# Two-network graph kernel on one core: the first LayerNorm with nodes on partitions, every reciprocal on columns of 25, the last LayerNorm's scale applied where be1 is added

## The chip, the core and the metric

One core of a Trainium2 chip. Five engines work side by side and meet by semaphores: TensorE (PE, matmul; its weight loads are listed as PEld), VectorE (DVE), ScalarE (ACT), GpSimd (POOL) and SyncE (SP, which here issues DMAs). SBUF and PSUM have 128 partitions. The metric is the device time of one execution in microseconds, the median of the runs.

## The reference

3125 nodes, 53125 edges sorted by destination, 128 features, all in float32. Cut to what is computed:

```
h = relu(layernorm(x))                                   # (x - mean) / sqrt(var + 1e-5), per node
for l in 1, 2, 3:                                        # three SAGE layers
    agg = segment_sum(h[src], dst) / max(count, 1)
    h = agg @ Wl.T + bl + h @ Wr.T                       # relu after layers 1 and 2
x = x + h
h = relu(layernorm(x))
messages = gelu((h[src] + edge_attr) @ We1 + be1) @ We2 + be2
u = (1 + eps) * h + segment_sum(messages, dst)
x = x + (gelu(u @ Wu1 + bu1) @ Wu2 + bu2)
```

## The kernel before

Node data lie transposed, features on the 128 partitions and the 3125 nodes along columns, in 7 chunks: six of 500 nodes and one of 125. A chunk has four blocks of 125 nodes (the last chunk has one), 25 blocks in all. Where rows of nodes are needed, 125 partitions hold one block.

The program has three stages.

**Build.** The dense matrix of edge counts `adj` (source node on partitions in blocks, destination along columns, 8 bits) is made from one-hots. 213 slots (`GB`) of two tiles of 125 edges each: DVE writes four one-hots (`key_onehots`, L444 to L459), PE multiplies them (`sum_group`, L720), ACT copies the result to `adj` (`keep_block`, L653). Before the first slot DVE works out the keys of all 425 tiles in ten operations (L429 to L442) that need `src_idx`, `dst_idx` and `firsts`. One-hots have 5 buffers, so DVE can be four slots ahead of PE; what DVE does in slot s of the plan is set against PE's slot s - 5 (`LEAD`).

**Dense layers.** A SAGE layer's sum over neighbours is `parts` (h as three bfloat16 parts, rows of nodes) times `adj`: 75 matmuls for each layer and chunk (`dense_unit`, L801). An order written out in `Plan` says in which slot each step of each chunk is issued on its engine. The first layer's matmuls are set among the slots of the build, 2.3 to a slot (`RATE`), from slot 38 on; after the build a slot is just nine of them. The result is multiplied by the reciprocal of the node's edge count (`mean_rows`, L492), mixed with weights on PE (`mix_layer`, L774), passed through ReLU on ACT (`activate`), turned by PE (`turn`, L753), and split: the high part by ACT (`split_high`, L673), the remainder by DVE (`split_rest`, L478), the middle and lowest parts by POOL (L402 to L405).

The counts: for each chunk SP stores the last partition's row of `adj` to DRAM and loads it as 25 rows (L354 to L360, with a wait between), PE sums it into all 128 partitions (`count`, L766), and DVE clips it and takes the reciprocal of [128 x 500] (`reciprocal_counts`, L485).

Both norms run on the transposed data: PE subtracts the mean by a matmul (`centre`, L737), ACT squares, PE averages the squares into all partitions (`variance`, L748), ACT takes the root, DVE the reciprocal of [128 x 500] and then max(., 0) times it (`normalise`, L470). The first norm is in slots 2 to 34 of the build. The last norm follows the third layer chunk by chunk: PE's `mix_rows` (h @ We1, rows of nodes, L788) waits for it, DVE adds `be1` (`keep_rows`, L509), and SP stores the rows to the `table` in DRAM (L365 to L370).

**Edges.** 85 groups of 625 edges. Once the table is stored, POOL gathers its rows with five indirect DMAs per group (L409 to L416), with 4 buffers: from group 4 on it waits for DVE's `pre` of four groups back. PE multiplies the edge features by We1, DVE adds the gathered rows (`pre`, L639), ACT takes GELU, DVE makes the window's one-hots, PE sums into the nodes (L895). Ahead of group 0 DVE runs checks of the input (`check_input`), which wait for the two loads of `order` (L371, L372) that SP issues right behind the table stores. PE waits for these checks at group 0 too. When a chunk's edges are done, `node_mix`, `node_sum`, `node_up`, `node_down` and `node_add` make its output.

## Time and profile before

| | |
|---|---|
| median of 3 runs | 1102.52 us (1101.01 to 1102.76) |
| the profiled execution | 1104.38 us, its span 1102.3 us |
| PE busy | 861.3 us, 78% of the span |
| DVE busy | 466.2 us, 42% |
| POOL busy | 443.8 us, 40% |
| ACT busy | 233.8 us, 21% |
| moved by DMA | 63.01 MB |

The span runs from the first to the last instruction; what lies around it is 2.1 us. Shares over the whole span mix the three stages, so they are to be read by stretches: the page cuts the span into 40 slices of 27.6 us and gives each engine's busy share in tenths. Operations of one engine overlap a little: the duration of one is longer than the distance from its start to the next one's start.

A row of a timeline gives the start, the duration (both us), the engine, the line of the kernel, the operation with output <- input, and in brackets the engine's idle time before it and what ended that. A row of a group gives line, engine, operation, shapes and count, then the busy time of all (us) and the mean of one (ns), then the idle time of the engine just before them. A row of a DMA queue gives packets, MB and the time they took as a share of 16 engines over the stretch.

### The profile page before, as it was taken

The numbers are of one execution on the slowest core, as the hardware profiler recorded it, in microseconds if no ns is written. First come the engines' busy times: TensorE is split into PE (matmuls) and PEld (weight loads), VectorE is DVE, ScalarE is ACT, GpSimd is POOL, SyncE is SP. The second block draws the span as 40 slices with busy tenths as digits, with TensorE's granted clock in tenths as the row PEclk, the third lists the DMA queues.
The fourth block names the chain that finished last, engine by engine and source line by source line (L and its number), as shares of the span: only waits on it lengthen the run. The fifth ranks groups of instructions, "written<-read, shape, count | busy, mean of one in ns | idle before, by whom it ended". The sixth has DMA issues, their size and how long they took to land.

```text
span 1102.3 us, 13178 instructions
## 1 busy us (share of the span) xinstructions
PE 861.3 (78%) x4419; PEld 601.1 (55%) x4419; DVE 466.2 (42%) x1522; ACT 233.8 (21%) x378; POOL 443.8 (40%) x483
## 2 busy tenths in 40 slices
PE   2658898999999998878756687586687687677576
PEld 1334454445544454434456686575676676666475
DVE  5999999994100012232363223223323323323221
ACT  1535666663100000000101111111111111111111
POOL 1110000000010100000077777777777777777773
PEclk9867999999999999998856557758657658567756
DMA  4000000001000000000033333333334333334321
GB/s 118 0 1 2 2 3 2 2 2 48 1 1 1 1 1 10 10 9 11 16 102 107 111 96 113 111 100 120 99 100 120 100 100 120 104 107 119 101 76 38
DMA packets 34768, 63.01 MB, mean 57 GB/s; under 512 B 10189, under 2 KB 16891, under 8 KB 34696
## 3 DMA queue, kind: packets, MB, share of 16 engines
q1 hardware_dynamic: 19224, 32.24, 9.8%
q0 software_dynamic: 13600, 27.88, 8.8%
q10 hardware_dynamic: 1872, 1.99, 0.6%
q8 instruction: 37, 0.61, 0.2%
q14 instruction: 35, 0.29, 0.1%
HBM read 58.80 MB, written 3.28 MB: 56 GB/s over the span
## 4 chain that ended last, share of the span: by engine, by line
POOL 36%; PE 34%; DVE 14%; issue 12%; DMA 2%; ACT 1%; POOLq 0%; SPq 0%; ACTq 0%; DVEq 0%
POOL f_adj L413 36%; PE f_ps L813 24%; DVE f_region L454 2%; PE f_ps L733 2%; DVE f_region L473 2%; DVE f_work L473 2%; DVE f_region L458 2%; PE f_ps L726 2%; DVE f_region L452 2%; DVE f_rcntT L490 1%; PE f_ps L785 1%; PE f_ps L786 1%; DVE f_region L456 1%; DMA f_adj<-in_firsts 1%; PE f_ps L797 1%
## 5 line engine op out<-in xcount | busy, mean ns | idle before, releaser
L413 POOL DMA_INDIRECT f_adj<-table,f_src_idx x425 | 403.7, 950 | 283.3 <-DMA table<-f_region 154.1
L813 PE MATMUL f_ps<-f_adj,f_parts 125*128 125x500 fp8e4 (+1 forms) x1575 | 341.2, 358 | 0.0
L895 PE MATMUL f_ps<-f_adj 125*128 125x101 f32 (+19 forms) x1020 | 207.0, 375 | 144.0 <-ACT f_adj L713 144.0
L895 PEld LDWEIGHTS f_ps<-f_adj 125*128 125x128 f32 x1020 | 192.8, 288 | 169.4 <-issue 168.9
L813 PEld LDWEIGHTS f_ps<-f_adj,f_parts 125*128 125x128 bf16 x1575 | 145.6, 99 | 136.6 <-issue 22.3
L554 DVE TENSOR_SCALAR f_adj<-f_iota,f_dst_abs 125x101 f32<-125x101 f16 (+3 forms) x425 | 87.0, 291 | 264.8 <-PE f_ps L895 264.7
L844 PE MATMUL f_ps<-f_We,f_region 128*125 128x128 f32 x850 | 178.4, 384 | 0.5 <-DVE f_region L514 0.5
L844 PEld LDWEIGHTS f_ps<-f_We,f_region 128*125 128x125 f32 x850 | 167.0, 294 | 0.7 <-issue 0.7
L403 POOL CAST f_parts<-f_rest 125x512 bf16<-125x512 f32 (+1 forms) x21 | 12.4, 590 | 356.6 <-DVE f_rest L483 356.6
L713 ACT ACTIVATE f_adj<-f_adj 125x640 f32<-125x640 f32 x85 | 62.6, 736 | 422.1 <-DVE f_adj L639 422.1
L659 ACT CAST f_adj<-f_ps 128x500 f32 x213 | 125.9, 591 | 86.1 <-PE f_ps L733 75.1
L639 DVE TENSOR_TENSOR f_adj<-f_ps,f_adj 125x640 f32<-125x640 f32 x85 | 69.8, 821 | 90.9 <-issue 69.6
L726 PE MATMUL f_ps<-f_region 125*128 125x300 f16 (+1 forms) x213 | 67.1, 315 | 39.7 <-DVE f_region L458 38.9
L733 PE MATMUL f_ps<-f_region 125*128 125x375 f16 x212 | 72.8, 343 | 0.0
L454 DVE TENSOR_SCALAR f_region<-f_iota,f_key 125x375 f16<-125x375 f16 x212 | 71.8, 338 | 0.0
L452 DVE TENSOR_SCALAR f_region<-f_iota,f_key 125x300 f16<-125x300 f16 x212 | 65.1, 307 | 5.9 <-PE f_ps L733 5.2
L726 PEld LDWEIGHTS f_ps<-f_region 125*128 125x128 f16 x213 | 21.8, 102 | 75.4 <-issue 47.4
L458 DVE TENSOR_SCALAR f_region<-f_iota,f_low 125x126 f16<-125x126 f16 x213 | 60.9, 286 | 0.0
L499 DVE TENSOR_TENSOR f_work<-f_ps,f_rcntT 128x500 f32<-128x500 f32 (+1 forms) x21 | 13.2, 627 | 109.4 <-PE f_ps L813 109.3
L456 DVE TENSOR_SCALAR f_region<-f_iota,f_low 125x126 f16<-125x126 f16 x212 | 56.8, 268 | 0.0
L483 DVE TENSOR_TENSOR f_rest<-f_ps,f_parts 125x512 f32<-125x512 f32 (+1 forms) x21 | 13.3, 631 | 62.4 <-ACT f_parts L678 62.4
L730 PE MATMUL f_ps<-f_region 125*128 125x25 f16 x212 | 39.1, 185 | 0.0
(108 smaller groups left out, 423.9 us busy)
## 6 DMA issues: line engine op xcount, KB each, us to landing
f_region<-in_edge_attr_T SPq DMA_DIRECT2D x85, 312.5 KB, 2.9
f_adj<-table,f_src_idx POOLq DMA_INDIRECT x425
f_xT<-in_xT ACTq DMA_DIRECT2D x6, 250.0 KB, 6.8
table<-f_region SPq DMA_DIRECT2D x6, 250.0 KB
out<-f_xT SPq DMA_DIRECT2D x6, 250.0 KB, 2.1
f_adj<-in_firsts SPq DMA_DIRECT2D x1, 415.0 KB
...
```

The lines of the kernel that those rows point to most:

```text
L413: pool.indirect_dma_start(out=rows[:, g % RW, j * D:(j + 1) * D], out_offset=None, in_=table, in_offset=bass.IndirectOffsetOnAxis(ap=src_i ...
L452: dve.tensor_scalar(keys[0:EP, slot, 0:s.A_COLS], iota[0:EP, 0:s.A_COLS], key[0:EP, tt:tt + 1], None, ALU.is_equal)
L454: dve.tensor_scalar(keys[0:EP, slot, s.A_COLS:KEYS], iota[0:EP, s.B_FROM:s.DW * NB], key[0:EP, tt + 1:tt + 2], None, ALU.is_equal)
L458: dve.tensor_scalar(lows[0:EP, slot, 0, 0:EVEN], iota[0:EP, 0:EVEN], low[0:EP, tt:tt + 1], None, ALU.is_equal).then_inc(onehots, 1)
L554: ins = dve.tensor_scalar(onehot[0:EP, g % OH, j, 0:hi - lo], iota[0:EP, 0:hi - lo], float(lo), dst_abs[0:EP, g * T + j:g * T + j + 1], AL ...
L639: dve.tensor_tensor(pre[0:EP, g % PM, :], z_group(g), rows[0:EP, g % RW, :], ALU.add).then_inc(pre_ready, 1)
L659: act.copy(adj[:, :, bass.ds(base, s.DW)], ps[:, build_ps(g):build_ps(g) + s.DW * NB].rearrange("p (w b) -> p b w", b=NB)).then_inc(kept, 1)
L726: pe.matmul(ps[:, o:o + wide], lows[0:EP, slot, 0, :], keys[0:EP, slot, 0:wide], start=True, stop=g == 0, skip_group_check=True)
L733: ins = pe.matmul(ps[:, o + s.B_FROM:o + s.DW * NB], lows[0:EP, slot, 1, :], keys[0:EP, slot, s.A_COLS:KEYS], start=False, stop=True, skip ...
L813: ins = pe.matmul(ps[:, dense_ps(i):dense_ps(i) + width(c)], parts[0:NP, (l % 2) * 3 + p, b, :], adj[0:NP, b, lo:hi].bitcast(F8), start=b ...
L844: ins = pe.matmul(z_ps(g, j), ea[:, g % EA, j * EP:(j + 1) * EP], weights["We1"][:, :], start=True, stop=True)
L895: ins = pe.matmul(agg_ps(c, lo, hi), msg[0:EP, g % PM, j * D:(j + 1) * D], onehot[0:EP, g % OH, j, at_lo:at_lo + hi - lo], start=opens and ...
```

## The change

- The first norm is made on rows of nodes. ACT's queue loads x as rows ([125 nodes] x 25 blocks) in two DMAs, of 12 and 13 blocks, into the part of `parts` that the second layer uses later; `xT` is loaded behind the weights. DVE takes each block's mean and variance (`bn_stats`, `bn_aggr`, two blocks to a slot from slot 0), ACT one Sqrt of [125 x 25], DVE one reciprocal of it and the shift, ACT one Relu with scale and shift for each block (from slot 9). The high part is a copy of these rows, PE turns them into PSUM, and ACT copies them to `hT` (`keep_turned`). The first remainder is taken by POOL instead of DVE.
- The keys are worked out for the first 54 tiles ahead of slot 0 and for the other 371 in slot 1. `firsts` is loaded second instead of fourth.
- Counts are summed by PE onto 125 partitions, one column per block. DVE clips and inverts [125 x 4]. SP stores that to DRAM node by node, waits, and loads it broadcast to 128 partitions; `mean_rows` waits for this load.
- Last norm: ACT writes `hT` as Relu of the centred values, without the scale. The variance comes out as one column per block, Sqrt and reciprocal are of [125 x 4], and the scale is applied to the rows where `be1` is added (four operations per chunk instead of one). `rows` is due one slot sooner. For the node update the scale is stored to DRAM, loaded broadcast (1.6 MB, SP, ahead of the two `order` loads), and multiplied into h by `node_scale` in edge groups 3 to 9.

```diff
         for c in range(s.NC):
-            a = 2 + 4 * c
-            self.put("cent", a, c)
-            self.put("square", a + 1, c)
-            self.put("var", a + 2, c)
-            self.put("std", a + 3, c)
-            self.put("norm", self.dve(a + 3), c)
-            self.turn(self.dve(a + 3) + 1, c)
+            ready = std + 1 + s.blocks(c)[-1]
+            self.put("high", ready, c)
+            self.put("turn", ready + 1, c)
+            self.put("keep", ready + 1, c)
...
-                self.put("norm", o + 2, m)
-                self.put("rows", o + 3, q)
-                self.put("rows_add", o + 3, q)
+                self.put("inv", o + 2, q)
+                self.put("rows", o + 2, q)
+                self.put("rows_add", o + 2, q)
...
                 sp.dma_start(c25[0:NB, lo:hi], counts[:, lo:hi]).then_inc(count_in[q % 2], 16)
+                sp.wait_ge(rcnt_ready, q + 1)
+                sp.dma_start(in_nodes(inv, q).rearrange("(b p) -> p b", p=NP), columns(cinv, q),
+                             allow_slow_non_contiguous=True).then_inc(inv_out, 16)
+                sp.wait_ge(inv_out, 16 * (q + 1))
+                sp.dma_start(at(rcntT, q), in_nodes(inv, q).partition_broadcast(P)).then_inc(rcnt_in[q % 2], 16)
...
+            sp.dma_start(inv.rearrange("(b p) -> p b", p=NP), rstd[0:NP, :],
+                         allow_slow_non_contiguous=True).then_inc(rstd_out, 16)
+            sp.wait_ge(rstd_out, 16)
+            sp.dma_start(rstdT[:, :], inv.partition_broadcast(P)).then_inc(rstd_in, 16)
             sp.dma_start(order[0:EP, 0, :], t["dst_rows"]).then_inc(order_in, 16)
             sp.dma_start(order[0:EP, 1, :], t["dst_next"]).then_inc(order_in, 16)
...
-                pool.wait_ge(rest_ready, j + 1)
+                if l == 0:
+                    pool.wait_ge(high, j + 1)
+                    pool.tensor_tensor(rest_rows(j), h_rows(c), part(0, 0, c), ALU.subtract).then_inc(rest0, 1)
+                    pool.wait_ge(rest0, j + 1)
+                else:
+                    pool.wait_ge(rest_ready, j - NC + 1)
...
+            def moments_of(b):
+                if b in (0, HALF):
+                    dve.wait_ge(x_in[b // HALF], 16)
+                dve.bn_stats(stats[0:NP, b, :], x_rows[0:NP, b, :]).then_inc(moment, 1)
+                dve.wait_ge(moment, b + 1)
+                dve.bn_aggr(moments[0:NP, b, :], stats[0:NP, b, :]).then_inc(made0, 1)
+
+            def invert0():
+                dve.wait_ge(std0_ready, 1)
+                dve.reciprocal(std0[0:NP, :], std0[0:NP, :]).then_inc(scaled0, 1)
...
-                dve.reciprocal(spread(m), spread(m)).then_inc(inverted, 1)
-                dve.wait_ge(inverted, m + 1)
-                dve.scalar_tensor_tensor(out=at(hT, c), in0=ps[:, cent_ps(m):cent_ps(m) + width(c)], scalar=0.0,
-                                         in1=spread(m), op0=ALU.max, op1=ALU.mult).then_inc(normed, 1)
+            def invert(c):
+                dve.wait_ge(std_ready, c + 1)
+                dve.reciprocal(columns(rstd, c), columns(rstd, c)).then_inc(inverted, 1)
...
-                dve.reciprocal(at(rcntT, q), at(rcntT, q)).then_inc(rcnt_ready, 1)
+                dve.reciprocal(columns(cinv, q), columns(cinv, q)).then_inc(rcnt_ready, 1)
...
-                    dve.wait_ge(rcnt_ready, c + 1)
+                    dve.wait_ge(rcnt_in[c % 2], 16 * (c // 2 + 1))
...
+                for i, b in enumerate(s.blocks(c)):
+                    ins = dve.scalar_tensor_tensor(
+                        out=grows[0:NP, c % 2, i * D:(i + 1) * D],
+                        in0=ps[0:NP, rows_ps(c) + i * D:rows_ps(c) + (i + 1) * D], scalar=rstd[0:NP, b:b + 1],
+                        in1=be1[0:NP, :], op0=ALU.mult, op1=ALU.add)
+                ins.then_inc(rows_kept, 1)
...
+            def node_scale(c):
+                if c == 0:
+                    dve.wait_ge(rstd_in, 16)
+                dve.scalar_tensor_tensor(out=at(uT, c), in0=at(hT, c), scalar=col["eps1"][:, 0:1], in1=at(rstdT, c),
+                                         op0=ALU.mult, op1=ALU.mult).then_inc(h_scaled, 1)
...
+            def normalise0(b):
+                act.wait_ge(scaled0, 2)
+                act.activation(x_rows[0:NP, b, :], x_rows[0:NP, b, :], ACT.Relu, bias=shift0[0:NP, b:b + 1],
+                               scale=std0[0:NP, b:b + 1]).then_inc(normed0, 1)
```

## Rows read from the trace of the kernel before

**Rows 1.** The page's slices: DVE's busy share in tenths.

```profile
DVE  5999999994100012232363223223323323323221
```

**Rows 2.** Stretches, core 0: time, PE, PEld, DVE, ACT, POOL busy, PE clock, DMA share, GB/s.

```profile
140.00:180.00 40.00, 37.19 (x235) 20.02 (x234) 39.10 (x175) 26.21 (x45) 1.76 (x2) 0.98 0.01 2
...
415.00:536.00 121.00, 106.53 (x497) 52.28 (x496) 29.59 (x24) 6.32 (x10) 0.00 (x0) 0.94 0.04 11
```

**Rows 3.** The page's group of gathers, and the timeline where the edge stage starts.

```profile
L413 POOL DMA_INDIRECT f_adj<-table,f_src_idx x425 | 403.7, 950 | 283.3 <-DMA table<-f_region 154.1
...
558.45 2.13 POOL L413 DMA_INDIRECT f_adj<-table,f_src_idx  x1 [0.30 <-issue]
...
559.18 0.58 DVE L604 TENSOR_TENSOR f_adj<-f_adj 125x425 f32<-125x425 int32 x1
...
564.87 0.82 DVE L639 TENSOR_TENSOR f_adj<-f_ps,f_adj 125x640 f32<-125x640 f32 x1
```

**Rows 4.** Timeline in the build, and the page's group of dense matmuls.

```profile
89.00 1.46 PE L813 MATMUL f_ps<-f_adj,f_parts 125*128 125x500 fp8e4 x3
...
115.16 0.60 ACT L659 CAST f_adj<-f_ps 128x500 f32 x1 [0.16 <-PE f_ps L733]
115.47 0.29 PE L726 MATMUL f_ps<-f_region 125*128 125x300 f16 x1
...
116.20 0.29 PE L726 MATMUL f_ps<-f_region 125*128 125x300 f16 x1
...
L813 PE MATMUL f_ps<-f_adj,f_parts 125*128 125x500 fp8e4 (+1 forms) x1575 | 341.2, 358 | 0.0
```

**Rows 5.** Groups by form on DVE, 0 to 560 us.

```profile
L454 DVE TENSOR_SCALAR f_region<-f_iota,f_key 125x375 f16<-125x375 f16 x212 | 71.8, 338 | 0.0
L458 DVE TENSOR_SCALAR f_region<-f_iota,f_low 125x126 f16<-125x126 f16 x213 | 60.9, 286 | 0.0
L490 DVE RECIPROCAL f_rcntT<-f_rcntT 128x500 f32<-128x500 f32 x6 | 19.7, 3278 | 0.2
...
L514 DVE TENSOR_TENSOR f_region<-f_ps,f_be 125x128 f32<-125x128 f32 x1 | 0.3, 292 | 0.9 <-PE f_ps L797 0.9
```

**Rows 6.** Timeline where POOL's two operations on a chunk meet DVE's one-hots.

```profile
61.99 0.67 DVE L454 TENSOR_SCALAR f_region<-f_iota,f_key 125x375 f16<-125x375 f16 x1
62.63 1.21 POOL L405 TENSOR_TENSOR f_parts<-f_rest,f_parts 125x512 bf16<-125x512 f32 x1
62.74 1.15 DVE L458 TENSOR_SCALAR f_region<-f_iota,f_low 125x126 f16<-125x126 f16 x1
```

**Rows 7.** Timeline of the kernel's start.

```profile
14.38 0.60 DVE L435 TENSOR_TENSOR f_adj<-f_adj 125x425 f32<-125x425 int32 x1 [6.68 <-DMA f_adj<-in_firsts]
```

**Rows 8.** DMA queues in 3:4, 14:15, 548:551 (packets, MB, share), and one stretch.

```profile
q10 hardware_dynamic: 161, 0.29, 81.8%
...
q1 hardware_dynamic: 173, 0.00, 12.1%
...
q1 hardware_dynamic: 342, 0.18, 22.3%
...
549.00:550.00 1.00, 0.43 (x2) 0.44 (x2) 0.48 (x2) 0.52 (x1) 0.00 (x0) 0.50 0.33 87
```

**Rows 9.** Timeline of a count's way through DRAM, and PE at the last chunk.

```profile
253.40 0.69 SPq L357 DMA_DIRECT2D counts<-f_adj  x1
...
255.63 0.26 SPq L360 DMA_DIRECT2D f_c<-counts  x1
...
282.75 0.30 PEld L785 LDWEIGHTS f_ps<-f_work,f_W1l 128*128 128x128 f32 x2 [0.33 <-DVE f_work L499]
```

**Rows 10.** Timeline of one chunk of the last norm.

```profile
445.42 2.07 PE L797 MATMUL f_ps<-f_We,f_hT 128*125 128x128 f32 x8 [2.89 <-DVE f_hT L475]
```

**Rows 11.** Timeline at the end of the last norm.

```profile
550.39 0.29 DVE L514 TENSOR_TENSOR f_region<-f_ps,f_be 125x128 f32<-125x128 f32 x1 [0.88 <-PE f_ps L797]
...
553.15 1.12 POOL L413 DMA_INDIRECT f_adj<-table,f_src_idx  x1 [154.06 <-DMA table<-f_region]
```

264 lines of the change are left out of this document (162 added, 102 removed).

## The prediction

> **What bounds the kernel now.** I read the slices first, then stretches, then groups, then the rows where two engines meet. VectorE (DVE) is busy nine tenths from 20 to 260 us and two to three tenths later [rows 1]. So there are three stages. In the build (17.6 to 257 us, 213 slots of one-hots) DVE has almost no idle time, and TensorE (PE) is close behind, 37.19 of 40 us [rows 2]. In the dense stage (257 to 534) PE never rests, except that from 415 to 536 it is busy only 106.53 of 121 us [rows 2]. In the edge stage (553 on) GpSimd (POOL) issues 425 gathers of 950 ns with 0.30 us between, 425 x 1.255 = 533 us [rows 3]. Whatever is saved ahead of the gathers moves their start; whatever POOL loses afterwards is lost for good.
>
> How close the three engines are in the build decides the worth of the change. A slot with two dense matmuls takes PE 116.20 - 115.47 = 0.73 us [rows 4], a dense matmul 0.21 (341.2 / 1575) [rows 4], so a slot without any takes 0.31 and one with the planned 2.3 takes 0.79. ScalarE (ACT) copies a block in 0.60 and waits 0.16 for itself: 0.76 [rows 4]. DVE's four one-hots go at 0.76 too: they overlap, so the spacing counts and not the 338 and 286 ns of one [rows 5]. DVE is late only because of its other work.
>
> **The change, part by part.**
>
> *Out of DVE in the build.* Seven norms (six wide ones with a reciprocal of 3.28, as L490's [rows 5], + 0.6 scale, one of 1.2): 24.6. Seven first splits, 6 x 0.60 + 0.3: 4. Five count reciprocals, 3.28 [rows 5] + 0.6 each: 19.4.
>
> *Into DVE.* The key arithmetic of the other 371 columns moves behind slot 1: ten operations of 0.34 to 0.54 with a wait between, 4.7. Per block of 125 nodes one bn_stats on 128 columns and one bn_aggr. No row shows either; the nearest are a 125x128 operation at 0.29 [rows 5] and an overhead of about 0.15, with a bound of 0.3 and 0.7 for the pair. I take 0.49, nearest to the 0.29 row: 25 x 0.49 = 12.2. Inverting 25 columns costs 0.4, and DVE waits about 2 for ACT's Sqrt and its table load. Five small count reciprocals: 1.4.
>
> *POOL against DVE.* While POOL's cast ran from 61.94, a DVE one-hot of the 338 ns kind took 0.67; while its subtraction ran from 62.63, one of the 286 ns kind (0.25 beside nothing) took 1.15 [rows 6]. That is 0.36 + 0.89 = 1.25 lost per chunk now. The change gives POOL a second subtraction in each of seven chunks: 6.25 x 0.89 = 5.6 more. The later splits (at 133, 166, 199, 231 us) now lie beside a DVE reciprocal that loses nothing; that cover goes with the reciprocals, 4 x 1.25 = 5. The Trainium skill (SBUF — State Buffer, Who interferes with whom) says that a 2-port DVE operation and a GpSimd operation exclude each other for a whole instruction; rows 6 agree.
>
> *Start.* Now DVE waits until 14.38 for `firsts` [rows 7] and sends the first one-hot at 17.6. With 54 columns ahead of it, that would come about 5 us sooner. But slot 0 then waits for node rows: 1500 pieces of 512 B from a transfer of 125 rows. When the table is stored, also 125 rows, the DMA share is 0.33, five engines of sixteen, and one 512 B piece takes 0.223 x 16 x 3 / 342 = 31 ns [rows 8]. So 300 x 31 = 9.3 us, beside `firsts` and `dst` (622 KB, at 83 GB/s 7.5): x arrives at 1.9 + 16.8 = 18.7, and the gain is spent. I take 0, between -5 and +5. The Trainium skill (DMA: Bandwidth & Descriptors, Why a DMA increments its semaphore by 16 and not by 1) says that a transfer runs on the largest number up to 16 that divides its outer dimension, which is 5 for 125; the 0.33 agrees.
>
> *Slots 0 to 38.* DVE: -24.6 - 4 + 4.7 + 12.2 + 2.4 + 5.6 = -3.7, so **-4**. In slots 9 to 33 ACT has 0.60 + a block's Relu (0.34) + a quarter of two copies (0.3) = 1.24 against DVE's 0.76 + 0.54 = 1.30: it is just beside the path.
>
> *Slots 38 to 213.* Now 256.5 - 89.0 [rows 4] = 167.5 us. DVE alone would lose 19.4 - 1.4 - 5 = 13. But PE's own sum is 175 x 0.31 + 388 x 0.21 + 5 mixes of 1.7 + turns and counts 3 + 5 at the low clock + 4.5 where no dense matmul is due = 157 to 158. So **-9.5**; bounds -13 and -4.
>
> *Counts through memory.* A reciprocal now goes out of SBUF and back, broadcast, before `mean_rows`. For chunks 0 to 4 that has 24 slots of cover. For the last chunk there is none: before, PE waits 0.33 [rows 9]. A small store and its wait took 255.63 - 253.40 = 2.23 [rows 9]; the load is taken at the same 2.2 to 2.9; less 1.0 of DVE's time saved, 3.8. Chunk 5 (500 pieces of 4 B, five engines) is late by about 1.2. Behind the waiting `mean_rows` stands PE's mix. **+5**, between 2 and 8.
>
> *Last norm.* In each of five chunks PE waits 2.89 for `normed`, behind the reciprocal of 3.28 [rows 10]. After the change `hT` is ready two ACT operations (0.59 + 0.68) after `cent`, and PE has nine dense matmuls and `var` in between. 5 x 2.89 = 14.4; `var` as eight loads with one column costs some 0.6 more, 3. **-11.4**, bounds -14.4 and -9.
>
> *Tail.* From PE's `cent` of chunk 5 at 536.95 the chain runs to the last kept rows at 550.39 + 0.29 [rows 11]. With the change, by the durations of the same stretch: square 538.7, Relu 539.4, var 540.1, mix 540.9, rows of chunk 5 542.8, cent 543.2, square and Relu 544.0, rows 544.6, kept 544.9. **-5.7**. Then 2.5 to the first gather, as now [rows 11].
>
> *The last scale's round trip.* SP stores `rstd`, 3125 pieces of 4 B, waits, broadcasts 1.6 MB, and only behind that stand the two `order` loads, for which DVE waits before it touches any edge group. With s the start of the gathers: POOL's group 4 needs the first `pre`, at s + 25.1 (20 x 1.255); now that is done at 564.87 + 0.82 = s + 12.5 [rows 3]. So 12.6 are covered. A 4 B load took 0.121 x 16 / 173 = 11 ns [rows 8], a 512 B store 31; no row shows a 4 B store. I take 20: 625 x 20 x 1.35 (the gathers take 35% of the DMA engines) = 17. Then: store issued s - 1.9, its pieces from s - 1.2, all there and seen s + 17.3; broadcast (a 1.8 KB piece took 0.818 x 16 / 161 = 81 ns [rows 8], 100 KB per engine, shared) 6.5, s + 23.8; order 7, s + 30.8; DVE's checks 5 and one-hots 1, `pre` 0.8, s + 37.5. **+12**; at 11 ns 4.5, at 31 ns 21.
>
> *The scale of h on DVE.* Seven operations with both inputs in SBUF, off DVE's path, but at 558.45 a gather took 2.13 instead of 0.94 when such a one (L604) began at 559.18 [rows 3]. Between 0 and 7 x 1.2; **+3**. `node_sum`, of the same size, costs nothing new.
>
> **Sum.** -4 - 9.5 + 5 - 11.4 - 5.7 + 12 + 3 = -10.6. Against the profiled execution (span 1102.3, 1104.38 in all) that is a span of 1091.7; against the median of the runs, 1102.52, it is 1091.9.
>
> **The rivals.**
>
> *A. The order loads arrive in time.* If a 4 B store costs what a 4 B load does, most of the 12 is covered: 1091.9 - 8 to - 12, about 1082. For: 11 ns measured. Against: it was a load, on sixteen engines.
>
> *B. Slower: the 4 B store.* The place is SP's queue between the last table store and `order`. Everything else sums to -22.6, and the store costs 12 + 0.84 per ns over 20, so from 33 ns per piece the kernel is slower. At 40 ns it is +6, 1109. For: a 512 B store already takes 31. Against: that one moves 128 times the bytes. The Trainium skill (DMA: Bandwidth & Descriptors, Specifications and Rules for kernel authors) says that below 512 B the engine reads, changes and writes back, and that a strided last dimension gives one descriptor per element; that speaks for B.
>
> *C. The reciprocals were hidden.* PE at 0.79 and ACT at 0.76 take over the whole build and the 13.5 of the build don't come: 1105. For: 37.19 of 40. Against: DVE has no idle time, and PE waits for it.
>
> *D. The change doesn't do what it says.* Excluded: reciprocals of 500 columns of 3.28 leave, 24.6 + 19.4 + 20 us of DVE.
>
> **How the numbers follow.** Forecast 0.48, A 0.27, B 0.15, C 0.10. Three runs lie within 0.2% (2 us), so less than that is no change. Faster: 0.45 of the forecast's, all of A, a little of C: 0.73. Same: 0.08. Slower: B and half of C: 0.19. Range: the low end is A with the build at its best bounds, 1075; the high end reaches B's 1108.
>
> **What would show it.** Right: the build ends near 243; PE waits 3 to 5 us at the mix of the last chunk of layer 0; no PE wait ahead of `mix_rows`; gathers begin near 528; POOL then idle once, some 12 us, at its 21st gather, with the first `pre` behind the `order` loads. Wrong: gathers evenly spaced throughout (A), that gap above 22 us (B), a build still near 240 us long (C), or DVE held at slot 0 past 20 us by the node rows.

## The result: 1073.9 us, 2.55% faster

Four runs of the changed kernel have a median of 1073.93 us (1072.47 to 1075.15), four runs of the kernel before beside them 1102.1. The ratio is 0.9745, 95% interval 0.9728 to 0.9762. The profiled execution has a span of 1070.8, that of before 1102.3. I had forecast 1091.9, from 1075 to 1108: the direction is right, the gain is nearly three times the forecast and the time lies 1.1 us below the range. Medians and ratios here and below are of the fast runs alone; one execution of `e3_order_first`, 2483.49 us long, is left out.

The two traces, cut at the same events (us). The forecast of each stage is the prediction's own term.

| stage | before | after | change | forecast |
|---|---|---|---|---|
| start to the first dense matmul | 89.00 | 79.25 | -9.75 | -4 |
| to the last matmul of the build | 167.5 | 152.0 | -15.5 | -9.5 |
| to the mix of layer 0's last chunk | 26.3 | 43.1 | +16.8 | +5 |
| to `cent` of chunk 5, last norm | 254.2 | 233.6 | -20.6 | -11.4 |
| to the last kept rows | 13.44 | 5.79 | -7.65 | -5.7 |
| to the first gather | 2.76 | 5.20 | +2.4 | 0 |
| to the last gather | 531.99 | 534.58 | +2.6 | +15 |
| sum, in the span | | | -31.5 | -10.6 |

### The profile page after: what moved, and what is told of

The parts are those of the page before. It is cut to its first block, busy times and chain, and to the rows that moved or that the text cites. A ratio compares the mean times of both kernels' runs of the same rounds, so it can differ in the third digit from the quotient of the medians.

```text
span 1070.8 us, 13339 instructions
## 1 busy us (share of the span) xinstructions
PE 833.0 (78%) x4445; PEld 588.4 (55%) x4445; DVE 417.7 (39%) x1581; ACT 240.5 (22%) x404; POOL 452.9 (42%) x490
## 3 DMA queue, kind: packets, MB, share of 16 engines
q1 hardware_dynamic: 26666, 35.47, 12.8%
## 4 chain that ended last, share of the span: by engine, by line
PE 36%; POOL 33%; issue 11%; DVE 11%; DMA 6%; ACT 1%; POOLq 0%; SPq 0%; ACTq 0%; DVEq 0%
POOL f_adj L450 33%; PE f_ps L913 25%; DVE f_region L508 2%; PE f_ps L830 2%; DVE f_region L504 2%; DVE f_region L506 2%; PE f_ps L823 2%; PE f_ps L887 2%; DMA f_parts<-in_x 2%; PE f_ps L888 2%; DVE f_region L510 2%; PE f_ps L995 1%; DMA inv<-f_rstd 1%; DMA inv<-f_cinv 1%; DMA f_adj<-in_dst_next 1%
## 5 line engine op out<-in xcount | busy, mean ns | idle before, releaser
L913 PE MATMUL f_ps<-f_adj,f_parts 125*128 125x500 fp8e4 (+1 forms) x1575 | 333.2, 353 | 0.0
L944 PE MATMUL f_ps<-f_We,f_region 128*125 128x128 f32 x850 | 173.7, 377 | 0.8 <-DVE f_region L563 0.8
L944 PEld LDWEIGHTS f_ps<-f_We,f_region 128*125 128x125 f32 x850 | 162.7, 287 | 0.9 <-issue 0.9
L440 POOL CAST f_parts<-f_rest 125x512 bf16<-125x512 f32 (+1 forms) x21 | 12.6, 598 | 291.0 <-DVE f_rest L530 290.5
L504 DVE TENSOR_SCALAR f_region<-f_iota,f_key 125x300 f16<-125x300 f16 x212 | 67.5, 319 | 5.1 <-PE f_ps L830 4.7
L506 DVE TENSOR_SCALAR f_region<-f_iota,f_key 125x375 f16<-125x375 f16 x212 | 69.3, 327 | 0.0
L508 DVE TENSOR_SCALAR f_region<-f_iota,f_low 125x126 f16<-125x126 f16 x212 | 63.9, 301 | 0.0
L510 DVE TENSOR_SCALAR f_region<-f_iota,f_low 125x126 f16<-125x126 f16 x213 | 57.8, 271 | 0.0
L776 ACT ACTIVATE f_hT<-f_ps,f_b 128x500 f32<-128x500 f32 (+1 forms) x14 | 8.9, 634 | 134.5 <-PE f_ps L888 134.5
```

What stands on the lines that cost most here:

```text
L504: dve.tensor_scalar(keys[0:EP, slot, 0:s.A_COLS], iota[0:EP, 0:s.A_COLS], key[0:EP, tt:tt + 1], None, ALU.is_equal)
L506: dve.tensor_scalar(keys[0:EP, slot, s.A_COLS:KEYS], iota[0:EP, s.B_FROM:s.DW * NB], key[0:EP, tt + 1:tt + 2], None, ALU.is_equal)
L508: dve.tensor_scalar(lows[0:EP, slot, 1, 0:EVEN], iota[0:EP, 0:EVEN], low[0:EP, tt + 1:tt + 2], None, ALU.is_equal)
L510: dve.tensor_scalar(lows[0:EP, slot, 0, 0:EVEN], iota[0:EP, 0:EVEN], low[0:EP, tt:tt + 1], None, ALU.is_equal).then_inc(onehots, 1)
L913: ins = pe.matmul(ps[:, dense_ps(i):dense_ps(i) + width(c)], parts[0:NP, (l % 2) * 3 + p, b, :], adj[0:NP, b, lo:hi].bitcast(F8), start=b ...
L944: ins = pe.matmul(z_ps(g, j), ea[:, g % EA, j * EP:(j + 1) * EP], weights["We1"][:, :], start=True, stop=True)
```

## The profile after

The page's slices, DVE busy and PE clock in tenths. DVE's nines end one slice sooner than in [rows 1]. The clock is low in the edge stage, and a little in the slice from 268 to 294 us, where PE waits for the last counts. The nines ahead of 83 us are not a measurement: after's clock records begin there, and the page counts the time without them as full clock.

```profile
DVE  4899999960000001111345232323323323323321
...
PEclk9999999999899999999757668558658558757656
```

Stretches of after: time, then busy time of PE, PEld, DVE, ACT, POOL, PE clock, DMA share, GB/s. The first answers to [rows 2]: PE, and no longer DVE, is the fuller of the two in the build. The second lies in the last norm: PE never rests and keeps its full clock, where before had 93.43 of 105 at a mean clock of 0.95. The two group rows are PE's wait for the one-hots from the first dense matmul to the end of the build, in before and in after.

```profile
140.00:180.00 40.00, 39.19 (x250) 21.13 (x249) 38.58 (x184) 27.54 (x48) 1.86 (x2) 1.00 0.08 9
395.00:500.00 105.00, 105.00 (x508) 53.45 (x507) 13.61 (x35) 6.65 (x15) 0.00 (x0) 1.00 0.05 13
...
L726 PE MATMUL f_ps<-f_region 125*128 125x300 f16 x173 | 51.9, 300 | 13.3 <-DVE f_region L458 12.7 <-ACT f_adj L659 0.4
...
L823 PE MATMUL f_ps<-f_region 125*128 125x300 f16 x174 | 51.0, 293 | 2.1 <-DVE f_region L510 1.4
```

The timeline of the start, and of the first dense matmuls (answers to [rows 4, 7]). Three of them take 1.46 us at first, as in before, and 0.79 from 83.64 on. The one-hots of slot 0 go at 15.08, and only behind them does DVE wait for the node rows, until 18.12 (forecast 18.7).

```profile
15.08 0.29 DVE L504 TENSOR_SCALAR f_region<-f_iota,f_key 125x300 f16<-125x300 f16 x1
...
18.12 0.29 DVE L485 BATCH_NORM_STATS2 f_stats<-f_parts 125x6 f32<-125x128 f32 x1 [2.20 <-DMA f_parts<-in_x]
18.45 0.18 DVE L487 BATCH_NORM_AGGREGATE f_moments<-f_stats 125x2 f32<-125x6 f32 x1
...
79.25 1.46 PE L913 MATMUL f_ps<-f_adj,f_parts 125*128 125x500 fp8e4 x3
...
83.64 0.79 PE L913 MATMUL f_ps<-f_adj,f_parts 125*128 125x500 fp8e4 x3
```

The timeline of the last two chunks' counts (answers to [rows 9]), in order of time: SP's store of the reciprocals, its broadcast load, DVE's `mean_rows`, PE's mix. The brackets are what to read. PE stands for 4.40 and 10.43 us behind DVE, which stands behind the load. Between SP's store and its next DMA lie 6.24 us for 500 pieces of 4 B and 6.06 for 125.

```profile
242.41 0.26 SPq L385 DMA_DIRECT2D inv<-f_cinv  x1
248.65 0.36 SPq L388 DMA_DIRECT2D f_rcntT<-inv  x1
253.23 0.68 DVE L546 TENSOR_TENSOR f_work<-f_ps,f_rcntT 128x500 f32<-128x500 f32 x1 [10.84 <-DMA f_rcntT<-inv]
253.96 2.04 PE L887 MATMUL f_ps<-f_work,f_W1l 128*128 128x500 f32 x2 [4.40 <-DVE f_work L546]
262.45 0.25 SPq L385 DMA_DIRECT2D inv<-f_cinv  x1
268.51 0.35 SPq L388 DMA_DIRECT2D f_rcntT<-inv  x1
274.03 0.29 DVE L546 TENSOR_TENSOR f_work<-f_ps,f_rcntT 128x125 f32<-128x125 f32 x1 [11.61 <-DMA f_rcntT<-inv]
274.37 0.79 PE L887 MATMUL f_ps<-f_work,f_W1l 128*128 128x125 f32 x2 [10.43 <-DVE f_work L546]
```

The timeline where the edge stage starts (answers to [rows 3, 11]): the store of `rstd` at 514.43, SP's next DMA 12.6 us later, DVE's checks at 539.94 when `order` is there, the first `pre` at 545.66, and POOL's one gap, at its 21st gather.

```profile
513.75 0.35 DVE L563 SCALAR_TENSOR_TENSOR f_region<-f_ps,f_rstd,f_be 125x128 f32<-125x128 f32 x1
514.43 1.07 SPq L399 DMA_DIRECT2D inv<-f_rstd  x1
518.95 1.32 POOL L450 DMA_INDIRECT f_adj<-table,f_src_idx  x1 [126.56 <-DMA table<-f_region]
527.03 0.34 SPq L402 DMA_DIRECT2D f_adj<-inv  x1
539.94 0.60 DVE L668 TENSOR_TENSOR f_adj<-f_adj 125x425 f32<-125x425 int32 x1 [17.36 <-DMA f_adj<-in_dst_next]
545.66 0.82 DVE L704 TENSOR_TENSOR f_adj<-f_ps,f_adj 125x640 f32<-125x640 f32 x1
546.75 0.94 POOL L450 DMA_INDIRECT f_adj<-table,f_src_idx  x1 [2.74 <-DVE f_adj L704]
```

## The experiments

The ratios are to the kernel before, run beside each. The batches of `e1_counts_wide` to `e8_keys_early` found it at 1102.7 and 1103.1. Three later batches (`e9_best` to `e18_rows`) ran on chips where every kernel took longer, before too (1228 to 1229); their ratios are uncertain by 0.34 to 0.67%. The difference is in the edge stage: with SP's extra DMAs (`e10_probe`) the first dense matmul is at 79.58 and the first gather at 519.67, in after at 79.25 and 518.95, but from there the gathers take 645 us. From those batches I use the times up to the first gather, and ratios.

**All counts the old wide way (`e1_counts_wide`).** After, with the count in a row on all partitions again, no store and no load:

```diff
+    WIDE = (0, 1, 2, 3, 4, 5, 6)
...
+                if q in plan.WIDE:
+                    continue
...
+                if q in plan.WIDE:
+                    dve.tensor_scalar(at(rcntT, q), ps[:, COUNT_PS:COUNT_PS + width(q)], UNIT, None,
+                                      ALU.max).then_inc(clipped, 1)
+                    dve.wait_ge(clipped, q + 1)
+                    dve.reciprocal(at(rcntT, q), at(rcntT, q)).then_inc(rcnt_ready, 1)
+                    return
```

> The changed kernel with the counts of all seven chunks handled as before: PE sums them into 128 partitions, DVE clips and inverts [128 x 500], nothing goes through DRAM. Theory 1 (DVE bounds the build when it has wide reciprocals, and the round trip stops PE for 14.8 us behind the build): slots 38 to 213 grow from 152 by 8 to 13 us (18 us more on DVE, less the 4.3 us of port losses that the reciprocals cover again), the stretch up to the mix of the last chunk of layer 0 shrinks from 43 to about 26. Net -4 to -9, about 1066 to 1070. Theory 2 (DVE's four slots of lead hide a 3.9 us reciprocal each time): the first stretch grows by no more than 3, net -14, about 1060.

Ratio 0.9703 (0.9683 to 0.9723), 1070.27 us. The build ends at 246.2 instead of 231.3, the mix of the last chunk comes at 272.43 instead of 274.37, with no wait. PE waits 13.3 us for the one-hots in the build again, as in before (2.1 in after). So the small reciprocals buy 14.9 in the build, more than either theory said, and the way through memory costs 16.8 up to the mix. It costs 1.7 more behind it: the last norm's stage takes 231.9 us here and 233.6 in after, where the clock is still low behind the late mix (0.52 from 274.4 to 278). 16.8 + 1.7 - 14.9 = 3.6, and the first gather comes at 515.33, 3.6 sooner than in after.

```profile
L834 PE MATMUL f_ps<-f_region 125*128 125x300 f16 x173 | 51.8, 299 | 13.3 <-DVE f_region L513 13.3
```

**Only chunks 5 and 6 wide (`e2_last_counts_wide`).** The same edit for q in (5, 6).

> The changed kernel with only the counts of the last two chunks (5 and 6) handled as before; chunks 0 to 4 keep their way through DRAM. Theory 1 (PE stands still for 4.4 + 10.4 us only because the reciprocals of these two chunks come back late from DRAM, and DVE is idle there anyhow): PE's waits ahead of the two mixes shrink to 0.3 us as in the kernel before, and the time falls by 15 to 17 us, to about 1057 to 1059. Rival (something else is late next, the remainder parts of chunk 5 and 6 for the second layer or the count itself): part of it stays, a fall of less than 8 us.

Ratio 0.9568 (0.9552 to 0.9585), 1055.97 us: 18 below after, more than expected. The build ends at 230.9 as in after, and from there to the mix it takes 26.3 us, which is what before took. The whole +16.8 is the last two chunks' way through memory, and most of the rest of the 18 is the low clock behind it: the last norm's stage takes 232.4 instead of 233.6. In the trace the mix stands right behind DVE:

```profile
255.83 0.94 DVE L541 RECIPROCAL f_rcntT<-f_rcntT 128x125 f32<-128x125 f32 x1
256.86 0.29 DVE L557 TENSOR_TENSOR f_work<-f_ps,f_rcntT 128x125 f32<-128x125 f32 x1
257.20 0.48 PE L905 MATMUL f_ps<-f_work,f_W1l 128*128 128x125 f32 x2
```

**One row stored instead of 4 B pieces (`e11_row_store`).** After, counts of chunks 5 and 6 inverted wide, and then

```diff
-                sp.dma_start(in_nodes(inv, q).rearrange("(b p) -> p b", p=NP), columns(cinv, q),
-                             allow_slow_non_contiguous=True).then_inc(inv_out, 16)
+                if q >= 5:
+                    sp.dma_start(in_nodes(inv, q).rearrange("(a n) -> a n", a=1), wide[0:1, (q - 5) * CHUNK:(q - 5) * CHUNK + width(q)]
+                                 ).then_inc(inv_out, 16)
+                else:
+                    sp.dma_start(in_nodes(inv, q).rearrange("(b p) -> p b", p=NP), columns(cinv, q),
+                                 allow_slow_non_contiguous=True).then_inc(inv_out, 16)
```

> The kernel after, but the counts of chunks 5 and 6 are inverted wide ([128 x 500], [128 x 125]) and still go through memory: one partition's row is stored as one piece of 2000 or 500 B instead of 500 or 125 pieces of 4 B, and then loaded broadcast as before. Theory 1 (the lateness is in pieces of 4 B: they are written in under 1 us, but SP sees them 4.7 us later): each store's way, from its issue to SP's next DMA, falls from 6.1 to about 2.3. PE's wait for the last chunk falls from 10.4 to 7.7 (10.4 - 3.7 + 0.9 for the wider clip and reciprocal), chunk 5's stays at 4.3 (- 3.8 + 3.6). About 1071. Theory 2 (any store of freshly made values here takes 6 us before SP sees it, whatever its pieces): the stores stay at 6.1, the waits grow to 8 and 11.3: about 1078. Theory 3 (the broadcast load is the larger half, held up by reading what was just written or 128 times the same bytes): the load's 4.5 and 5.4 stay in both cases.

```profile
245.20 0.21 SPq L387 DMA_DIRECT2D inv<-f_wide  x1
246.32 0.35 SPq L393 DMA_DIRECT2D f_rcntT<-inv  x1
...
258.06 0.21 SPq L387 DMA_DIRECT2D inv<-f_wide  x1
259.12 0.35 SPq L393 DMA_DIRECT2D f_rcntT<-inv  x1
...
263.89 0.79 PE L904 MATMUL f_ps<-f_work,f_W1l 128*128 128x125 f32 x2 [5.26 <-DVE f_work L557]
```

Theory 1, and stronger than I put it: the store's way falls from 6.1 to 1.1 us, PE's waits from 4.40 and 10.43 to 1.58 and 5.26. The broadcast load remains and is now the larger half, as theory 3 had it, but it became shorter too: 3.2 and 4.4 from issue to `mean_rows`, 4.6 and 5.5 in after. Ratio 0.969 (0.9647 to 0.9733), 40 us below before, where after is 28 below.

**Twelve DMAs measured one by one (`e10_probe`).** SP issues each where it is otherwise idle, and waits for it.

> The kernel after, with twelve extra DMAs on SP in the dense stage, where SP has nothing else to do, each waited for before the next. They write to and read from scratch memory of their own. Stores: 3125, 500 and 125 pieces of 4 B; 125 pieces of 8, 16, 100 and 512 B; one piece of 2000 B. Loads: those 2000 B broadcast to 128 partitions, the same again, 2000 B written longer ago broadcast, and 125 rows of 512 B. Measured is the time from one issue to the next. Theory 1 (a piece below some size is seen late, by about 4 us, beside 9 to 14 ns for each piece on its engine): 12, 6.2, 6.1 for the 4 B ones, 6 for 8 B, 4 to 6 for 16 and 100 B, 2.3 to 2.5 for 512 and 2000 B. Theory 2 (the number of pieces alone counts): 12, 3.5, 2.4, and 2.4 for all the stores of 125 pieces. Loads: if reading what was just written is what costs, 4.5 and then 2.5; if 128 reads of the same bytes cost, 4.5 three times and 2.5 for the rows. The kernel's time stays at 1073.9.

The timeline of SP; a store's way is the distance to the next row, and pieces are in the table below.

```profile
276.02 0.29 SPq L404 DMA_DIRECT2D pr<-f_std  x1
...
284.69 0.29 SPq L404 DMA_DIRECT2D pr<-f_std  x1
...
290.57 0.26 SPq L404 DMA_DIRECT2D pr<-f_std  x1
...
296.78 0.26 SPq L404 DMA_DIRECT2D pr<-f_std  x1
...
299.45 0.25 SPq L404 DMA_DIRECT2D pr<-f_std  x1
...
300.88 0.25 SPq L404 DMA_DIRECT2D pr<-f_std  x1
...
302.41 0.25 SPq L404 DMA_DIRECT2D pr<-f_ident  x1
304.37 0.21 SPq L404 DMA_DIRECT2D pr<-f_rcntT  x1
...
305.49 0.34 SPq L404 DMA_DIRECT2D f_spare<-pr  x1
```

| DMA | us |
|---|---|
| store, 3125 / 500 / 125 pieces of 4 B | 8.67 / 5.88 / 6.21 |
| store, 125 pieces of 8 / 16 / 100 / 512 B | 2.67 / 1.43 / 1.53 / 1.96 |
| store, one piece of 2000 B | 1.12 |
| load of 2000 B to 128 partitions: just written / again / written earlier | 3.35 / 3.39 / 3.03 |
| load of 125 rows of 512 B, to its last packet | about 1.9 |

Both theories miss in part. The number of pieces says little: 500 and 125 cost the same, and 3000 more, 600 on each of five engines, add 2.5 us to the 6.2, 4 ns a piece. 4 B pieces are seen late, but already 16 B are not. In the trace of DMA work the 125 pieces are moved between 291.3 and 291.6, 5.2 us before SP goes on. Reading what was just written costs nothing; 128 reads of the same bytes take 3.0 to 3.4 in any case. For the last load, behind which no DMA waits, only the packets can be read: they end 1.9 us after its issue, those of the first broadcast load 2.8.

**Order loads first (`e3_order_first`).** The two `order` loads stand ahead of the store of `rstd`.

> The changed kernel with SP's two loads of order issued ahead of the store of the last scale instead of behind its broadcast. Theory 1 (the first pre comes late only through these loads, and POOL loses just the 2.4 us by which that is later than its 21st gather needs it): the gap goes and the time falls by 2 to 3 us, to about 1071.4. Rival (the loads take five DMA engines from the store and the table, so the broadcast comes later and group 3 waits for it, or the gathers start later): no change.

Ratio 0.9701 (0.9684 to 0.9718), 1069.73 us, 4.2 below after where I expected 2 to 3. POOL's gap is gone, and the last gather comes 531.83 after the first, which is before's 531.99: 2.75 of the 4.2. Another 1.0 lies ahead of the gathers, where nothing was changed (the stage up to the last mix takes 41.5 us in this trace and 43.1 in after's). The store's own way becomes longer, 15.7 us, and DVE's `node_scale`, which needs it, has no wait. SP's rows:

```profile
514.54 0.81 SPq L401 DMA_DIRECT2D inv<-f_rstd  x1
530.20 0.35 SPq L404 DMA_DIRECT2D f_adj<-inv  x1
```

**The scale stored as rows (`e7_store_rows`).**

```diff
-            sp.dma_start(inv.rearrange("(b p) -> p b", p=NP), rstd[0:NP, :],
-                         allow_slow_non_contiguous=True).then_inc(rstd_out, 16)
+            sp.dma_start(inv.rearrange("(p b) -> p b", b=NB), rstd[0:NP, :]).then_inc(rstd_out, 16)
```

> The changed kernel with the last scale stored to DRAM as 125 pieces of 100 B, in the order partition, block, instead of 3125 pieces of 4 B; so h is scaled with the values of other nodes in the node update. Changed kernel: 12.6 us from issue to SP's next DMA. Theory 1 (the time is per piece, 625 on each of five engines): the store takes 2.3 to 3 us. Theory 2 (a store of pieces under 512 B has a fixed part of about 5 to 6 us, as the 6.05 us for the 125 pieces of 4 B of the last count chunk suggest): it takes about 6.

```profile
515.60 0.65 SPq L399 DMA_DIRECT2D inv<-f_rstd  x1
519.67 0.34 SPq L401 DMA_DIRECT2D f_adj<-inv  x1
```

4.07 us instead of 12.6, between the two theories, no gap of POOL, one run of 1071.47. The difference is 8.5 us. Spread over the 600 more pieces on each of five engines it would be 14 ns a piece, but 4.7 of it lie already between 125 pieces of 4 B and 125 of 100 B (`e10_probe`). That leaves some 4 us, an estimate of 6 ns a piece, where I had taken 20 x 1.35 = 27.

**The wait taken out of before (`e4_rows_later`), and put back into after (`e5_wait_back`).**

```diff
-                self.put("rows", o + 3, q)
-                self.put("rows_add", o + 3, q)
+                late = 5 if q < 5 else 3
+                self.put("rows", o + late, q)
+                self.put("rows_add", o + late, q)
```

```diff
+                    if c < 5:
+                        dve.wait_ge(normed, c + 1)
+                        dve.wait_ge(lowest, 3 * NC)
+                        dve.reciprocal(spare[0:NP, :], rest[0:NP, 0, 0:CHUNK]).then_inc(held, 1)
...
             def mix_rows(c):
+                if c < 5:
+                    pe.wait_ge(held, c + 1)
```

> The kernel before, with one edit: in the last norm the products with We1 of chunks 0 to 4 are due two slots later, so that 18 more dense matmuls stand between the variance and PE's wait for the norm. All reciprocals stay. Theory 1 (each wait of PE costs its 2.9 us and then a stretch at the 1.2 GHz level, in which the eight matmuls of mix_rows take 2.07 instead of about 1.0 us): the five waits go and the granted clock of 415 to 536 us rises from 0.94 to 1.00; the time falls by 19 to 21 us, to about 1082. Theory 2 (only the waits count): it falls by 14.4 us, to 1088.

> The changed kernel, with an additional reciprocal of [125 x 500] on DVE (its result is not used) in the last norm of chunks 0 to 4, for which mix_rows waits. It starts after the small reciprocal, so PE waits about 4 us in each of five chunks. Theory 1 (wait plus low clock): 5 x (4 + 1.3) = 26 us more, about 1100. Theory 2 (wait alone): 5 x 4 = 20 us more, about 1094.

`e4_rows_later`: 0.9794 (0.9775 to 0.9812), 1080.51 us; that stage takes 231.8 instead of 254.2. `e5_wait_back`: 0.9999 (0.9988 to 1.0011), 1103.43; it takes 265.1 instead of 233.6. The first removes waits of 14.4 us and gains 22.4; the second adds 18.7 and loses 31.5. Most of the rest is the clock: before's mean of 0.94 over 121 us [rows 2] is 7.3 us of the first one's 8.0, and 0.90 over the 132 us from 406 to 538 in `e5_wait_back` is 13 for the second one's 12.8. Stretches of `e4_rows_later`, then of `e5_wait_back`, whose second one lies right behind a wait, and that wait in its timeline:

```profile
395.00:500.00 105.00, 105.00 (x476) 50.64 (x475) 29.30 (x25) 6.58 (x11) 0.71 (x2) 1.00 0.04 10
```

```profile
395.00:500.00 105.00, 90.02 (x392) 46.19 (x391) 23.60 (x32) 5.31 (x12) 0.00 (x0) 0.90 0.04 10
...
439.00:446.00 7.00, 6.77 (x22) 3.69 (x23) 1.30 (x5) 0.00 (x0) 0.00 (x0) 0.56 0.13 34
```

```profile
439.23 2.07 PE L907 MATMUL f_ps<-f_We,f_hT 128*125 128x128 f32 x8 [3.74 <-DVE f_spare L599]
```

Eight matmuls take 2.07 us there and 1.04 in `e4_rows_later`. A mean of 0.56 is mostly the lower level, 1.2 GHz. Before showed it too: [rows 10] has 2.07 for the eight, and from 445.5 to 449 its clock is 0.53. I read the wait in that row and not the duration beside it.

**Six reciprocals put back (`e14_six_reciprocals`).** After, with this in six slots of the first norm:

```diff
+                if slot in (10, 14, 18, 22, 26, 30):
+                    dve.wait_ge(held, 1 + (slot - 10) // 4)
+                    dve.reciprocal(spare[:, :], spare[:, :]).then_inc(held, 1)
```

> The kernel after, with six extra reciprocals of [128 x 500] on DVE (3.28 us each, of a tile of ones that nothing uses) in slots 10, 14, 18, 22, 26 and 30 of the build. Theory 1 (DVE alone sets the pace of slots 0 to 38): the first dense matmul, at 79.25 in after, moves by the whole 6 x 3.28 = 19.7 to 99, and the end by about as much: 1093. Theory 2 (ACT, with a copy and a Relu in each of these slots, is level with DVE and hides part): 8 to 14 us later, 1083 to 1088.

The first dense matmul is at 90.56, 11.3 later, not 19.7: theory 2 in size, but only partly for its reason. DVE stays busy 10.00 of every 10 us from 50 to 90. What shrinks is its other work: the one-hots up to there take 51.1 us instead of 56.8, because POOL's subtractions now run beside a reciprocal. In after one holds up a one-hot for its whole length (first fence), beside a reciprocal nothing is lost (second). That is 5.7. Of the last 2.7, 2.5 are DVE's own waits for PE and for the node rows, 4.3 us in after and 1.8 here.

```profile
56.92 1.23 DVE L508 TENSOR_SCALAR f_region<-f_iota,f_low 125x126 f16<-125x126 f16 x1
...
56.92 1.18 POOL L436 TENSOR_TENSOR f_rest<-f_parts 125x512 f32<-125x512 f32 x1 [1.00 <-ACT f_parts L763]
```

```profile
55.52 3.26 DVE L582 RECIPROCAL f_spare<-f_spare 128x500 f32<-128x500 f32 x1
...
56.77 1.15 POOL L437 TENSOR_TENSOR f_rest<-f_parts 125x512 f32<-125x512 f32 x1 [2.92 <-ACT f_parts L769]
```

**The first remainder on DVE (`e6_rest_on_dve`), and the later keys in slot 0 (`e8_keys_early`).**

```diff
-                    pool.tensor_tensor(rest_rows(j), h_rows(c), part(0, 0, c), ALU.subtract).then_inc(rest0, 1)
...
+                dve.tensor_tensor(rest_rows(j), t_rows(c) if l else h_rows(c), part(l, 0, c), ALU.subtract).then_inc(rest_ready, 1)
```

```diff
-                if slot == 1:
+                if slot == 0:
                     edge_keys(HEAD, NT)
```

> The changed kernel with the first remainder of layer 0 (seven subtractions) taken by DVE instead of POOL. Theory 1 (POOL's subtraction costs DVE 0.9 us each time, because a one-hot waits for it): DVE gets 0.6 us of its own for each and loses 0.9 less, so slots 9 to 38 shrink by 1 to 3 us and the time by as much. Theory 2 (ACT's 0.51 us Relu for each block bounds slots 9 to 33, and DVE's losses are hidden behind it): no change, or up to 1 us more.

> The changed kernel with the keys of the other 371 tiles worked out in slot 0, ahead of the first wait for the node rows, instead of in slot 1 behind it. Theory (DVE idles 2.2 us in slot 0 until the rows of x are there at 18.1 us): the 4.9 us of keys fill that wait, and the time falls by 2.2 us. Rival (ACT or PE set the time of slots 9 to 38, or the second half of x comes too late for slot 6): no change.

Both bring the first dense matmul forward, to 76.82 and 76.94: -2.4 and -2.3, inside the expectation and on it. Ratios 0.9686 (0.9669 to 0.9704) and 0.9697 (0.9678 to 0.9716), 5.2 and 4.7 us below after in the medians. The excess over 2.4 isn't explained, but stages that an edit doesn't touch differ by as much between executions: from the end of the build to the last mix eight traces with the counts through memory take 41.1 to 43.1 us, and after's own is the longest; from `cent` of chunk 5 to that of chunk 6 it is 4.1 in one trace and 5.4 in another.

**All of it together.** Three edits (last counts wide, order first, keys early) ran twice, four (also the first remainder on DVE) three times, and a kernel with the order loads behind again and the scale stored as rows and read with a stride, so that each node gets its own scale, beside the other three edits, twice.

> The kernel after with three edits together: counts of chunks 5 and 6 the old wide way, the two order loads issued before rstd is stored, the keys of the 371 later tiles worked out in slot 0. Theory 1 (the three act in different places: the end of the build, SP's queue at the start of the gathers, the start): the gains add. 1055.97 (last counts wide) - 3.9 (order first) - 4.7 (keys early) = 1047.4. PE has no wait ahead of the mixes of chunks 5 and 6, POOL no idle gap at its 21st gather. Theory 2 (a clock that happened to be better, or one gap behind another, made part of the single gains): 1050 to 1053.

> The same three edits and, with them, the first layer's remainder on DVE instead of POOL. Theory 1 (while POOL subtracts, DVE's one-hot waits, and POOL is slow at it; alone it brought the first dense matmul 2.4 us forward): 2.4 to 3 below the three edits alone, about 1045. Theory 2 (in slots 9 to 38 ACT and DVE are level, and with the keys gone from slot 1 ACT is what is late): within 1 us of the three edits alone.

> The kernel after with three edits together: counts of chunks 5 and 6 wide, order loads ahead of the store of rstd, keys of the 371 later tiles in slot 0. Theory 1 (the gains add): 1047.4, 0.950 of before. First dense matmul at 77, first gather at 499, no idle gap of POOL at its 21st gather, last gather 532 after the first. Theory 2 (they overlap): 1050 to 1053, 0.953 to 0.955.

> The three edits and, with them, the first layer's remainder on DVE instead of POOL. Theory 1 (what POOL's subtraction does to DVE's one-hots is saved at the first dense matmul and reaches the end): 2.5 below the three edits, 1045, 0.9478 of before. Theory 2: the first gather comes 2.5 sooner, as in the trace that there is (496.2 against 498.9), but the edge stage gives it back: the same as the three edits.

> As the four edits, but the order loads stay behind the scale's load, and the scale is stored as 125 pieces of 100 B (node 125 b + p at p x 25 + b) and read by node_scale with a stride of 25 elements; the result is the reference's. Theory 1 (the 4 B pieces cost only through SP's queue, in which the order loads now stand ahead): store seen after 4.1 us instead of 12.6, no gap of POOL, and the same time as the four edits within 1 us, 1045. Theory 2 (3125 pieces of 4 B also slow the table's store and the gathers): 1 to 2 us less. Theory 3 (DVE reads with a stride of 100 B more slowly and holds up the edge groups 3 to 9, whose pre the gathers wait for): 2 to 5 us more.

> The four edits (counts of chunks 5 and 6 wide, order loads ahead of the store of rstd, keys of the 371 later tiles in slot 0, the first remainder on DVE). First gather at 495.6 to 496.2, as in both traces that there are. Theory 1 (the gains add on a chip whose edge stage takes 534 us): last gather 532 later, span 1044, 0.947 of before. Theory 2 (the edge stage gives part back): first gather the same, 0.951 or more.

> As the four edits, but the order loads stay behind and the scale is stored as 125 pieces of 100 B and read with a stride. Its first gather came at 494.7, 0.9 to 1.5 us before the four edits', because the table's store shares the queue with less; node_scale took 1.05 us instead of 0.67. Theory 1: 1 us faster than the four edits, 1043. Theory 2 (seven strided operations of 1.05 us hold up pre): 1 to 3 us slower.

| kernel | ratio to before (95%) | first gather |
|---|---|---|
| three edits (`e9_best`) | 0.9550 (0.9515 to 0.9585) | 498.85 |
| three edits (`e15_three_edits`) | 0.9623 (0.9576 to 0.9669) | 498.24 |
| four edits (`e12_best_rest`) | 0.9528 (0.9494 to 0.9562) | 496.19 |
| four edits (`e16_four_edits`) | 0.9538 (0.9472 to 0.9605) | 495.57 |
| four edits (`e17_four_edits`) | 0.9553 (0.9510 to 0.9597) | 496.29 |
| stored as rows (`e13_best_rows`) | 0.9564 (0.9502 to 0.9627) | 494.67 |
| stored as rows (`e18_rows`) | 0.9563 (0.9520 to 0.9606) | 494.64 |

Up to the first gather the gains add: 518.95 - 17.5 (last counts, at the first gather) - 3.1 (first remainder) - 2.9 (keys, both at the build's end) = 495.4, measured 495.6 to 496.3. At the end they could not be read: these are the slow edge stages, where all seven ratios lie between 0.953 and 0.962, and the same kernel differs from one batch to the next (three edits 0.9550 and 0.9623). Four edits have the lowest ratios, 0.953 to 0.955 of before and so 2% below after's 0.9745, but their intervals overlap with those of the others. A ratio to a before of 1229 us also understates a gain that lies ahead of the edge stage: in microseconds below before, after is at 28, `e2_last_counts_wide`, with one edit, at 47, and four edits at 54 to 58, uncertain by 4 to 8. POOL has no gap at its 21st gather in them; in the slow edge stage it waits later, 5.9 to 6.7 us between 538 and 543. Storing the scale as rows brings the first gather 0.9 to 1.7 us forward, and `node_scale` with its stride takes 1.05 us instead of 0.67; whether the sum gains stays open, and so does whether the forecast 1044 comes out where the edge stage is fast.

## Why the prediction was wrong, term by term

The sum of -10.6 was 20.9 us short of the trace's -31.5, and no single step did it. The gain was put too small in the edge stage by 12.4 (the scale's store priced per 4 B piece, and 3 for the scale of h), in the last norm by 9.2 (the low clock behind each wait put at nothing), in the build by 6.0 (PE's own sum too long), at the start by 5.8 and in the tail by 2.0. Against these stand the counts' way through memory, 11.8 dearer than forecast, and 2.4 ahead of the first gather. Without this opposite miss the time would lie further below the range.

**Slots 0 to 38, -4: measured -9.75.** The terms add up to -8.6 in DVE's work instead of -3.7. In the group of both moments below, 25 pairs take 11.5 us busy and stand 0.42 apart, not 0.49 (-1.8). The wait of 2 for ACT's Sqrt isn't there (-2). POOL's second subtraction added 4.5 to the one-hots (52.3 to 56.8), not 5.6 (-1.1). Keys (4.8 for 4.7) were right. The start gained 0.3, as "nothing" said. Before's DVE also waited 1.1 for ACT's root, which I had not counted and which is gone. ACT's Relu took 0.50 instead of 0.34 and ACT was busy 9.72 us from 50 to 60, but DVE 10.00: it stayed the bound. So adding up DVE's work comes out here (-8.6 - 0.3 - 1.1 = -10.0), but it need not: `e14_six_reciprocals` shows that six reciprocals are worth 11.3 in this stage and not their 19.7.

```profile
L485 DVE BATCH_NORM_STATS2 f_stats<-f_parts 125x6 f32<-125x128 f32 x25 | 6.9, 275 | 2.2 <-DMA f_parts<-in_x 2.2
L487 DVE BATCH_NORM_AGGREGATE f_moments<-f_stats 125x2 f32<-125x6 f32 x25 | 4.6, 182 | 0.9
```

**Slots 38 to 213, -9.5: measured -15.5.** PE is the bound, as forecast (39.19 of 40 us). DVE's share of the gain is there too: PE waited 13.3 us in this stage before, all but 0.6 of it for the one-hots, and 2.1 after. The other 4.3 are PE's own work, which took longer under the clock: in before it fell behind each of three waits of 2.43 (a mean of 0.57 from 138 to 142 us). What failed is PE's own sum of 157, for a stage that takes 152. Two of its terms are too large. The low clock at the start of the stage isn't gone: three dense matmuls take 1.46 us at 79.25 as they did at 89.00, and the first three slots last 4.4 us where the next three with as many matmuls take 2.4. So it costs 2.0, and I had added the whole 5 us. (`e2_last_counts_wide`, whose clock records begin sooner, has the low level there too, the stretch below.) And for slots without a dense matmul I had added 4.5, while all of PE's waits are 2.1. Together that is at least 5.4. `e1_counts_wide` shows that the gain is the reciprocals' doing, 14.9. Rival C, that they were hidden, is out.

```profile
75.00:80.00 5.00, 3.36 (x14) 1.57 (x15) 5.00 (x18) 2.71 (x6) 3.00 (x5) 0.50 0.00 0
```

**Counts through memory, +5: measured +16.8.** The largest miss of a single term, and of the sign that hurts. The mechanism was right: no cover at chunk 6, PE's mix behind the waiting `mean_rows`. Each of the sizes was too small: a store's way 6.06 instead of 2.2, because I took it from a count store whose pieces are longer [rows 9]; a load of 4.5 and 5.4 to its landing instead of 2.2 to 2.9 (that one was no broadcast; in a quiet queue a broadcast took 3.0 to 3.4); chunk 5 late by 4.40 instead of 1.2; and behind each wait PE at the low clock (the mix of chunk 5 takes 2.04, 1.06 in `e2_last_counts_wide`). Another 1.7 of this low clock falls into the next stage.

**Last norm, -11.4: measured -20.6.** Five waits of 2.89 are gone, 14.4, as forecast. I had deducted 3 for `var`, and it costs nearly nothing: `e1_counts_wide` has the new `var` and no late counts and takes 231.9 here, `e4_rows_later` with the old one 231.8. After's 1.8 more are the low clock behind the late mix. And I had left out the clock: 22.4 - 14.4 = 8 by `e4_rows_later`, 31.5 - 18.7 = 12.8 by `e5_wait_back`, whose waits are longer. So -14.4 - 8 + 1.8 = -20.6. The low clock behind a wait was put at nothing though [rows 2] has 0.94 for this stretch; `e4_rows_later` and `e5_wait_back` show its price from both sides.

**Tail, -5.7: measured -7.65**, then **+2.4 to the first gather, where I had 0.** They seem to belong together. With the tail shorter, chunk 5's table store (250 KB) is issued at 513.39, right behind its rows, and the first gather waits 5.56 for it; before it went out at 548.15, 5.00 ahead of its gather, and was hidden by the tail. That it is this store and not chunk 6's, or the pieces of the scale behind it in the same queue, no run separates; with the scale as rows (`e13_best_rows`) the wait behind the last kept rows is 5.0 instead of 5.2. Taken together -5.2, the forecast's -5.7.

**Order round trip, +12, and the h scale, +3: measured +2.6 for both.** The chain is as forecast, link by link: 21st gather, first `pre`, `order`, the scale's store. What was mis-sized is the store, and what was wrong about it is its price by the piece. It was seen at s + 8.1, not s + 17.3. Of these 9.2 us the store itself makes 6.6: from issue to seen it took 12.6, not 19.2, and some 5 of them don't depend on the number of pieces (`e10_probe`). The other 2.6 are s: the gathers began later behind the store, which went out at s - 4.5 and not at s - 1.9. So the gap is 2.7. That is rival A, though not for its reason, a cheap piece, alone. The h scale costs nothing: with the order loads first the gathers take 531.83. Rival B, slower from 33 ns a piece, is out. The rule of the Trainium skill (DMA: Bandwidth & Descriptors, Specifications) that I had let speak for B, that pieces under 512 B are read, changed and written back, isn't seen as a price here: 125 pieces of 16 B took 1.43 and of 512 B 1.96. What these runs show to be dear is the 4 B piece, and less so the one of 8 B (2.67).

Of what "would show it", PE's missing wait ahead of `mix_rows`, the late first `pre` and POOL's single gap came, the gap with 2.7 us instead of 12; PE's wait at the last mix was 10.43, not 3 to 5; the build ended at 231, not 243, and the gathers began at 519, not 528.
